# The last stage of a routed-experts kernel: its results loaded, summed and stored in six pieces instead of four, three of the sums on GpSimd

## The reference

```python
top_w, top_i = jax.lax.top_k(logits, K)                 # K = 2 experts of E = 8 for each token
gw = jax.nn.softmax(top_w, axis=-1).astype(xf.dtype)
combine = (gw[:, :, None] * jax.nn.one_hot(top_i, E, dtype=xf.dtype)).sum(axis=1)
...
for e in range(E):
    h = jax.nn.gelu(xf @ w1[e] + b1[e], approximate=False)
    out = out + combine[:, e:e + 1] * (h @ w2[e] + b2[e])
shared = jax.nn.gelu(xf @ ws1 + bs1, approximate=False) @ ws2 + bs2
return (out + shared).reshape(orig_shape)
```

## Time and profile before

| what | value |
| --- | --- |
| time, median of three runs | 870.53 us (869.16 to 872.47) |
| time of the profiled execution | 869.57 us |
| its span, from the first to the last instruction | 867.8 us |
| DVE busy | 618.4 us (71% of the span) |
| PE busy | 616.0 us (71%) |
| POOL busy | 458.5 us (53%) |
| ACT busy | 438.3 us (51%) |
| last scatter issued, first load issued, end of the last sum | 842.13 us, 844.37 us, 863.47 us |

### The profile page before, as it was taken

How to read it: one execution, slowest core, us unless ns; L and a number is a source line. 1 busy time by engine, 2 the same in 40 slices (tenths; PEclk the granted TensorE clock), 3 DMA queues, 4 the chain that set the end, 5 groups by cost and what they waited for, 6 DMA issues and landing times. The chain is left out here.

```text
span 867.8 us, 21824 instructions
## 1 busy us (share of the span) xinstructions
PE 616.0 (71%) x7762; PEld 451.0 (52%) x7762; DVE 618.4 (71%) x1397; ACT 438.3 (51%) x873; POOL 458.5 (53%) x591
## 2 busy tenths in 40 slices
PE   0569975780079999225799999989714795999950
PEld 0354433560069999212566666555402574999940
DVE  6997887683048888287688889888513873888846
ACT  5634457760035555171766676666603332555524
POOL 1238758887547777510002223464764880777760
PEclk9968987995579999755899999999956997999985
DMA  9610002351144464242122233342111512545418
GB/s 284 151 38 1 0 8 67 71 90 50 37 74 90 98 99 88 86 166 62 45 87 71 80 98 88 82 116 55 42 33 29 86 32 47 93 101 100 89 32 285
DMA packets 131850, 70.51 MB, mean 81 GB/s; under 512 B 89535, under 2 KB 118725, under 8 KB 131746
## 3 DMA queue, kind: packets, MB, share of 16 engines
q1 hardware_dynamic: 121042, 50.46, 25.1%
q0 software_dynamic: 9088, 16.88, 7.0%
q10 hardware_dynamic: 1616, 1.77, 0.7%
HBM read 26.61 MB, written 30.50 MB: 66 GB/s over the span
## 5 line engine op out<-in xcount | busy, mean ns | idle before, releaser
L1500 ACT ACTIVATE ARENA<-banks,ARENA 128x256 f32<-128x256 f32 x312 | 122.3, 476 | 97.1 <-PE banks L1460 94.6
L2227 DVE TENSOR_REDUCE ARENA<-banks 128x4 f32<-128x1024 f32 (+1 forms) x128 | 122.8, 959 | 32.5 <-PE banks L1970 29.5
L1458 PE MATMUL banks<-ARENA,W1H 128*128 128x256 f16 x312 | 87.2, 279 | 58.4 <-DMA ARENA<-slots 57.6
L1472 PE MATMUL banks<-W2L,ARENA 128*128 x624 | 110.0, 219 | 2.7 <-DVE ARENA L1513 2.3
L1473 PE MATMUL banks<-W2H,ARENA 128*128 x624 | 109.7, 219 | 0.1
L1474 PE MATMUL banks<-W2H,ARENA 128*128 x624 | 109.7, 219 | 0.0
L2150 ACT ACTIVATE ARENA<-banks 128x1536 f32<-128x1536 f32 x64 | 92.6, 1447 | 24.2 <-PE banks L1994 24.1
L1448 POOL DMA_INDIRECT expert_out_g<-ARENA x78 | 78.0, 999 | 46.6 <-issue 26.2
L1448 POOL DMA_INDIRECT expert_out_f<-ARENA x78 | 81.1, 1040 | 33.6 <-issue 23.9
L1532 DVE TENSOR_TENSOR ARENA<-ARENA 128x1024 f16<-128x1024 f32 x78 | 95.6, 1226 | 2.7
L1058 POOL DMA_INDIRECT slots<-ARENA,PLACE x64 | 77.0, 1204 | 26.0 <-issue 17.5
(11 more groups left out here) (324 smaller groups left out, 1731.3 us busy)
## 6 DMA issues: line engine op xcount, KB each, us to landing
spread<-ARENA SPq DMA_DIRECT2D x96, 64.0 KB
ARENA<-expert_out_f SPq DMA_DIRECT2D x8, 512.0 KB, 6.5
ARENA<-spread SPq DMA_DIRECT2D x16, 256.0 KB, 3.0
ARENA<-spread SPq DMA_DIRECT2D x32, 128.0 KB, 2.8
ARENA<-expert_out_g SPq DMA_DIRECT2D x8, 512.0 KB, 6.6
XT<-in_w SPq DMA_DIRECT2D x10, 256.0 KB, 7.7
slots<-EMPTY SPq DMA_DIRECT2D x16, 129.0 KB
ARENA<-in_w SPq DMA_DIRECT2D x8, 256.0 KB, 6.9
```

The costliest lines, as they stand in the source:

```text
L1458: pe.matmul(out, t.W1H[:, e, ms], XST[i][:, 0], start=True, stop=False)
L1472: pe.matmul(out, hh, t.W2L[:, e, m, :], start=(m == 0), stop=False)
L1500: ins = nc.scalar.activation(HF[i % 2][:, m], UP[i % 2][:, m], ACT.Gelu, bias=BIAS[i % 4][:, m:m + 1], scale=1.0 / WS)
L2227: dve.tensor_reduce(MX[:, G // 2, tile, :, :, G % 2].rearrange("p s a -> p a s"), src, AX.X, ALU.max).then_inc(m_red, 1)
```

## The change

The tail is cut into six pieces of tiles, `LAST` = (0, 2), (2, 8), (8, 16), (16, 24), (24, 28), (28, 32). Each piece has its own loads (one DMA for each half, so twelve instead of eight), its own weighing on ACT and DVE, its own sum and its own store (six instead of four). The sums of pieces 1, 2 and 4, counted from 0, are done by POOL instead of DVE. The bytes are the same. The memory is laid out as before. `routed_program` takes the list of pieces as an argument, and the attention stage passes it the four chunks that it had.

```diff
-        for c in range(NT // CT):
+        for i, (first, last) in enumerate(loads):
+            c, j = divmod(first, CT)
             for k in range(2):
-                sp.dma_start(BACK[c][:, k], rows[:, k, CT * c:CT * c + CT]).then_inc(back_in[c], 16)
+                sp.dma_start(BACK[c][:, k, j:j + last - first], rows[:, k, first:last]).then_inc(back_in[i], 16)
...
+LAST = ((0, 2), (2, 8), (8, 16), (16, 24), (24, 28), (28, 32))
+LAST_ON_POOL = (1, 2, 4)
...
+        def sums(k):
+
+            c, j = divmod(LAST[k][0], CT)
+            res = t.RES[:, LAST[k][0]:LAST[k][1], :]
+            return res, res, routed.BACK[c][:, 1, j:j + len(tiles(k))]
 
         @block.sync
         def _(sp):
             routed.sync(sp)
-            for c in chunks:
-                sp.wait_ge(back_added, c + 1)
-                sp.dma_start(store[:, CT * c:CT * c + CT, :], t.RES[:, CT * c:CT * c + CT, :]).then_inc(stored, 16)
-            sp.wait_ge(stored, 16 * NT // CT)
+            for k, (first, last) in enumerate(LAST):
+                if k in LAST_ON_POOL:
+                    sp.wait_ge(summed_pool, LAST_ON_POOL.index(k) + 1)
+                else:
+                    sp.wait_ge(summed, on_dve.index(k) + 1)
+                sp.dma_start(store[:, first:last, :], t.RES[:, first:last, :]).then_inc(stored, 16)
+            sp.wait_ge(stored, 16 * len(LAST))
 
         @block.gpsimd
         def _(pool):
             routed.gpsimd(pool)
+            for k in LAST_ON_POOL:
+                pool.wait_ge(first_added, k + 1)
+                pool.wait_ge(second_weighted, k + 1)
+                nc.gpsimd.tensor_tensor(*sums(k), ALU.add).then_inc(summed_pool, 1)
...
-            for c in chunks:
-                dve.wait_ge(routed.back_in[c], 32)
-                weigh_first(dve, t, routed, c, range(CT * c, CT * c + CT)).then_inc(first_added, 1)
-                dve.wait_ge(first_added, c + 1)
-                dve.wait_ge(second_weighted, c + 1)
-                res = t.RES[:, CT * c:CT * c + CT, :]
-                dve.tensor_tensor(res, res, routed.BACK[c][:, 1], ALU.add).then_inc(back_added, 1)
+            for k in range(len(LAST)):
+                dve.wait_ge(routed.back_in[k], 32)
+                weigh_first(dve, t, routed, LAST[k][0] // CT, tiles(k)).then_inc(first_added, 1)
+                if k not in LAST_ON_POOL:
+                    dve.wait_ge(first_added, k + 1)
+                    dve.wait_ge(second_weighted, k + 1)
+                    dve.tensor_tensor(*sums(k), ALU.add).then_inc(summed, 1)
```

More of the change, by code:

```diff
@@ L1346, in _, with routed_program @@
             merge_step(NG - 1)
-def routed_program(nc, t, tag, sem, back_at):
+def routed_program(nc, t, tag, sem, back_at, loads):
     part = Bag()
@@ L1380, in routed_program @@
         "up_mm", "hidden", "high", "split", "down_mm", "y_set"))
-    back_in, primed = [sem(f"back_in{i}") for i in range(NT // CT)], sem("primed")
+    back_in, primed = [sem(f"back_in{i}") for i in range(len(loads))], sem("primed")
     ps = t.psum
@@ L1575, in last_stage, with tiles @@
         sem = stage_semaphores(nc, ctx, "sg_")
[L1576 to L1579, removed]
+        routed = routed_program(nc, t, "g", sem, None, LAST)
+        first_added, second_weighted, stored = sem("first_added"), sem("second_weighted"), sem("stored")
+        on_dve = [k for k in range(len(LAST)) if k not in LAST_ON_POOL]
+        summed, summed_pool = sem("summed"), sem("summed_pool")
         block = ctx.enter_context(nc.Block())
+        def tiles(k):
+            return range(*LAST[k])
+        def sums(k):
+            c, j = divmod(LAST[k][0], CT)
+            res = t.RES[:, LAST[k][0]:LAST[k][1], :]
+            return res, res, routed.BACK[c][:, 1, j:j + len(tiles(k))]
         @block.sync
@@ L1601, in _ @@
             act.wait_ge(routed.weights_set, 2)
-            for c in chunks:
-                act.wait_ge(routed.back_in[c], 32)
-                weigh_second(nc, t, routed, c, range(CT * c, CT * c + CT)).then_inc(second_weighted, 1)
+            for k in range(len(LAST)):
+                act.wait_ge(routed.back_in[k], 32)
+                weigh_second(nc, t, routed, LAST[k][0] // CT, tiles(k)).then_inc(second_weighted, 1)
         @block.vector
@@ L1745, in attention_stage @@
         sem = stage_semaphores(nc, ctx, "a_")
-        routed = routed_program(nc, t, "f", sem, ARENA - BACK_WORDS)
+        routed = routed_program(nc, t, "f", sem, ARENA - BACK_WORDS, [(c, c + CT) for c in range(0, NT, CT)])
         middle = middle_program(nc, t, sem, routed)
```

## The result

The changed kernel takes 874.05 us (median of ten runs, 872.95 to 877.03) against 870.82 us for the kernel before in the same runs: the ratio is 1.0042, 95% interval 1.0026 to 1.0058. That is 3.2 us slower, less than 0.5% but clear of the interval, and just above the top of the range that was given (874.0).

What follows compares the result with a forecast made beforehand. Loads were taken to bound the tail's start and DVE its end. The last sum 2.3 us later, less 0.9 for a smaller last store, gave +1.4 us on 870.53: 871.9 us, range 867.5 to 874.0.

Steps and rivals of the forecast that it cites:

- the net of +1.4 us: Whole tail: last sum 2.3 us later, last store 0.9 us shorter, added to the median of 870.53 us.
- the end of the sum: Behind DVE's last sum: only the last store, then 1.5 us carried over, so the span ends 3.4 us after the sum.
- the last sum ends later by: End of DVE's work: the last sum at 865.75 instead of 863.47, 2.3 us later, with POOL's sums priced as DVE time.
- POOL and DVE one after the other: Tail's sums and weighings, all in SBUF: whole instructions take turns, POOL getting in between DVE's; chance 0.60, at 871.9 us.
- The first rival: POOL's sums run beside DVE, which then waits for loads; span 2.5 us shorter, 868.0 us; chance 0.15.
- POOL loses to DVE's stream: Second rival: gapless weighings keep POOL's sums waiting, in part or whole; 873.5 to 874.9 us; chance 0.13.
- The strict reading of the Trainium skill's words on issue order: POOL's sums against DVE's weighings: issue order decides who blocks, and the weighings are issued first, so POOL would wait.
- Loads: Start of the tail: twelve issues end at about 850.3 instead of 848.3; all but piece 1 land before DVE reaches them.
- The last store: End of the tail: 256 KB instead of 512 moves in 0.9 us less, by the rate of the slices.
- the estimate of 0.6 from the Trainium skill's fit: Halving the last store, at 2.0 us plus bytes at 436 GB/s per DMA, saves 0.6 us; net would be +1.7.
- A switch from its scatters costs POOL nothing: POOL's first sum in the tail: no visible cost, since one began 0.02 us after an indirect DMA.

Runs made afterwards that it cites:

- e6: Changed kernel with all six sums on DVE, POOL's drain moved ahead and two dead POOL sums reading SBUF: 875.09 us, ratio 1.0051 to the kernel before.
- e7: Changed kernel with all six sums on DVE, POOL's drain moved ahead and five dead POOL writes: 870.15 us, ratio 0.9995 to the kernel before.
- e8: Changed kernel with POOL's drain moved ahead and the residual copied by ACT to PSUM for DVE's weighings: 869.36 us, ratio 0.9996 to the kernel before.
- e1: Changed kernel with one drain added on POOL between its last scatter and first sum: 871.95 us, ratio 1.0012 to the kernel before.
- e2: Kernel before with a tiny POOL write added at the end of POOL's list, waiting for the last sum: 874.63 us, ratio 1.0046.
- e5: Kernel before with the same tiny POOL write, waiting for the first of the four sums instead: 870.16 us, ratio 0.9992.
- e9: Kernel before with a tiny POOL write after the last sum and a second drain after 40 of 78 scatters: 874.99 us, ratio 1.0055.

## Why the prediction was wrong

The range missed by 0.05 us; the net of +1.4 us that it was built on was under half of what came. The step that failed is the end of the sum: "Behind the last sum stands the store of chunk 3", from which the forecast took the end of the span as the last sum, a store, and 1.5 us that it carried over as they were, without asking what fills them. The block also ends with a barrier, and the barrier waits for each engine's closing drain. POOL's was in the trace of before, 10.89 us long and ending at 849.6, but the prediction never looked at what closes the lists. By giving POOL work at the end of the tail, the change moved that drain from under the wait for the loads to behind the last sum.

Term by term, in us:

| term | forecast | measured |
| --- | --- | --- |
| the last sum ends later by | +2.3 | 20.99 - 19.10 = +1.89 |
| from the last sum to the landing of the last store (3.2 before) | -0.9 | 869.2 - 866.90 = 2.3: -0.9 |
| from there to the end of the span (1.1 before) | 0 | 872.9 - 869.2 = 3.7: +2.6 |
| together | +1.4 | +3.6 |

The other steps:

- *POOL and DVE one after the other.* Right. The first rival (side by side) would have shown no weighing longer than 0.35 us; one took 2.28 and one 1.35 (some 2.6 and 1.5 forecast). e6 and e7 show that POOL's reads of SBUF are the cause, and e8 that it goes away when DVE has one input in PSUM. This is what the Trainium skill states in SBUF — State Buffer, Who interferes with whom: a Vector instruction with two SBUF inputs contends with a GpSimd instruction that reads SBUF, and not with one that only writes. The traces agree in each of the three: eight weighings took 4.27 us beside POOL's reads in e6, 2.19 beside its writes in e7, and 2.15 beside its reads with one input in PSUM in e8. Why POOL's small power operation of the earlier trace rows, which reads SBUF too, did not hold up the DVE operation beside it was not tried.
- *POOL loses to DVE's stream.* Wrong as a rival: POOL's sums took 1.80, 2.34 and 1.30 us, the last of them begun among back-to-back weighings. The strict reading of the Trainium skill's words on issue order was not borne out here: that sum took 1.30 us, 1.28 alone, and the weighing issued behind it waited.
- *Loads.* Piece 1 landed 5.61 us after the first issue (5.33 forecast), piece 2 at 8.99 (8.28). Twelve loads are somewhat slower than eight, but POOL's first sum held DVE less for it (2.41 us for piece 2's weighings against 2.18 alone, so 0.2 us instead of 0.8), and the two largely cancel. Piece 3 landed at 11.79, later than DVE was ready for it, which the prediction had ruled out: DVE has a gap of 0.38 us there, and POOL's second sum got in during that gap, not between two weighings. The last sum came 0.4 us earlier than forecast: the weighings of pieces 4 and 5 with POOL's sum over them took 3.19 us, where the sum had 865.05 - 861.45 = 3.6.
- *The last store.* Right at 0.9; the estimate of 0.6 from the Trainium skill's fit was the farther one.
- *A switch from its scatters costs POOL nothing.* True where it was looked at, between a scatter and the next sum. The price is paid at the drain.

That the drain sets the end is shown by e1 (taken away: 2.5 us of the tail back, and the median 0.9 us above the kernel before instead of 3.2) and by e2 with e5 (put in by itself: 3.1 us of the tail and 3.6 of the median). What is left of the change, e1 against before, is +1.0 us of the tail, within 0.4 us of the forecast sum, with the misses on the loads partly cancelling.

## What to carry to other kernels

Follow every engine's list to the barrier that closes its block before giving an idle engine work near the end: the span ends with the last closing instruction, not with the last store, and an engine that was idle may have been hiding a long one. If POOL has issued many indirect DMAs and must work late, drain it early, while it waits anyway; that is one instruction (e1). Where POOL does not wait, the early drain costs its whole length (e9). And a sum moved from DVE to POOL takes DVE's time as well, at nearly POOL's longer duration, where DVE's instruction beside it has two inputs in SBUF and POOL reads SBUF; put one of DVE's inputs into PSUM, or don't move the sum.

## What the runs showed of the hardware

A drain on POOL takes about 83 ns for each indirect DMA that POOL has issued since the drain before. The closing lines of the other three stages of the kernel before, whose POOL lists hold 64, 110 and 32 scatters, read:

```profile
L127 POOLq DRAIN  x1: 5292/5292/5292, 232.4 to 232.4; - x1
```

```profile
L1744 POOLq DRAIN  x1: 9041/9041/9041, 647.5 to 647.5; - x1
```

```profile
L1161 POOLq DRAIN  x1: 2672/2672/2672, 720.1 to 720.1; - x1
```

That is 82.7, 82.2 and 83.5 ns for one. In e2, e5 and e9 the drain's time takes in the tiny instruction of 98 ns ahead of it; the rest is 6458 / 78 = 82.8 ns in the first two and 3184 / 38 = 83.8 in e9. POOL's other instructions do not enter: these stages have 59, 241 and 7 of them, the last stage none. It does not matter how long ago the scatters landed: in the front stage POOL waits for all of them before it drains, and in e2 they had landed over 19 us earlier. Only the drain that follows directly on the other has next to nothing to do (the drain of line 105, right behind the barrier, takes 0.1 to 0.2 us). What the drain does for each of them was not tried.
